# Graph scatter stage: TensorE's bank addresses packed into one word per four pairs, ScalarE's loop over units turned by half a unit

## The reference, cut to what matters

```python
def _spmm(src, dst, w, x, n):
    return jax.ops.segment_sum(w[:, None] * x[src], dst, num_segments=n)
...
msg = h[src] * norm[:, None]
out = jax.ops.segment_sum(msg, dst, num_segments=n_nodes)
```

## Time and profile before

| | us |
|---|---|
| median of 3 runs (2047.58 to 2049.47) | 2048.79 |
| the profiled execution, its own time | 2048.91 |
| the profiled execution, its span | 2047.0 |
| building stage, TensorE's first pair to ScalarE's last instruction | 107.7 to 689.7 |
| TensorE busy over the span | 1791.3 (88%) |
| VectorE busy | 930.7 (45%) |
| ScalarE busy | 605.9 (30%) |

### The profile page before, as it was taken

The page is one execution under the profiler, slowest core; times in us unless marked ns, Lnnn a source line. Parts: engine busy times, 40 slices in busy tenths (PEclk is TensorE's granted clock), DMA queues, the critical chain, the costliest instruction groups (busy, mean ns, idle before and its releaser), DMA issues.

```text
span 2047.0 us, 31184 instructions
## 1 busy us (share of the span) xinstructions
PE 1791.3 (88%) x10360; PEld 1412.7 (69%) x10364; DVE 930.7 (45%) x1708; ACT 605.9 (30%) x1076; POOL 149.8 (7%) x163
## 2 busy tenths in 40 slices
PE   2588988888777799999999999979999999998992
PEld 1288888777676577777777777756667777676871
DVE  5899999788777101111103323332220332235343
ACT  0023567777777410000001111233320000004540
POOL 2000000000000000000000000000000000140354
PEclk8789999899898789999999999989999999999996
DMA  2041133333334854444444343400017434433554
GB/s 86 21 142 80 80 160 160 160 160 160 160 160 195 277 152 137 136 143 144 148 142 128 112 128 114 127 1 0 0 49 247 120 119 125 133 120 117 163 156 138
DMA packets 108624, 260.96 MB, mean 127 GB/s; under 512 B 13005, under 2 KB 65383, under 8 KB 103067
## 3 DMA queue, kind: packets, MB, share of 16 engines
q1 hardware_dynamic: 90874, 240.29, 34.4%
q0 software_dynamic: 5568, 12.82, 2.0%
q10 hardware_dynamic: 12128, 7.16, 1.5%
HBM read 160.44 MB, written 108.04 MB: 131 GB/s over the span
## 4 chain that ended last, share of the span: by engine, by line
issue 53%; PE 29%; ACT 7%; DVE 6%; ACTq 3%; POOL 1%; DMA 1%; DVEq 1%; SPq 0%; POOLq 0%
PE ps L1732 11%; PE ps L1798 5%; PE ps L1733 4%; ACT ps L711 3%; ACT wide L705 3%; PE ps L1993 2%; PE ps L2009 2%; ACTq L696 2%; DVE act_c L1195 1%; PE ps L1704 1%; PE ps L1815 1%; POOL act_c L1016 1%; PE ps L2001 1%; PE ps L1985 1%; DMA act_c<-expert_replies,pair_tab 1%
## 5 line engine op out<-in xcount | busy, mean ns | idle before, releaser
L1732 PE MATMUL ps<-early,act_c 128*128 128x200 bf16 x3600 | 473.0, 261 | 102.9 <-ACT ps L679 57.2
L1798 PE MATMUL ps<-wide 128*128 128x320 f32 (+1 forms) x2000 | 534.8, 428 | 2.9 <-DVE pair_tab L1435 2.9
L1798 PEld LDWEIGHTS ps<-wide 128*128 128x128 f32 x2000 | 379.3, 191 | 145.2 <-DVE pair_tab L1435 3.0
L1732 PEld LDWEIGHTS ps<-early,act_c 128*128 128x128 bf16 x3600 | 343.0, 101 | 135.4 <-issue 127.5
L1733 PE MATMUL ps<-early,act_c 128*128 128x208 bf16 x1200 | 316.6, 264 | 0.0
L1798 PE MATMUL ps<-wide,act_a 128*128 128x320 f32 (+1 forms) x1000 | 268.3, 431 | 8.8 <-ACTq L744 8.8
L1195 DVE TENSOR_TENSOR act_c<-act_c,pair_tab 128x3072 bf16<-128x3072 bf16 x150 | 262.3, 1749 | 0.0
L1798 PEld LDWEIGHTS ps<-wide,act_a 128*128 128x128 f32 x1000 | 192.0, 192 | 82.6 <-issue 11.8
L705 ACT COPY wide<-ps 128x816 f32<-128x816 f32 x200 | 167.1, 836 | 174.5 <-PE ps L1733 135.3
L1299 DVE TENSOR_TENSOR wide<-ps,rows 128x1280 f32<-128x1280 f32 x10 | 14.9, 1492 | 409.1 <-PE ps L1815 409.1
L711 ACT ACTIVATE ps<-ones 128x816 f32<-128x816 f32 x200 | 170.6, 853 | 8.1
(11 more groups left out here) (232 smaller groups left out, 1498.3 us busy)
## 6 DMA issues: line engine op xcount, KB each, us to landing
wide<-weight_matrix SPq DMA_DIRECT2D x90, 800.0 KB, 4.5
weight_matrix<-wide SPq DMA_DIRECT2D x20, 2000.0 KB, 6.2
count_matrix<-wide SPq DMA_DIRECT2D x20, 2000.0 KB, 10.8
wide<-count_matrix SPq DMA_DIRECT2D x45, 800.0 KB, 4.5
expert_replies<-wide SPq DMA_DIRECT2D x63, 128.0 KB, 1.9
wide<-weight_matrix SPq DMA_DIRECT2D x20, 400.0 KB, 3.7
rows<-routed_tokens SPq DMA_DIRECT2D x42, 128.0 KB, 2.3
wide<-count_matrix SPq DMA_DIRECT2D x10, 400.0 KB, 3.9
```

The source lines that it names most:

```text
L1732: nc.tensor.matmul(weights, hot_lane[:, slot, part, two, :, k], hot_key[:, slot, two, 0:WCOLS, k], start=False, stop=True, skip_group_chec ...
L1798: i = nc.tensor.matmul(ps[:, 2 * sub + h, 0:n], features[:, q * QUADS + t, h * P:(h + 1) * P], moving, start=q == 0 and t == 0, stop=q == ...
```

## The change

1. **TensorE's tables.** The 16 offsets and 4 free numbers of a line become 4 words, one for each quad: the free number in bits 0 to 8, and the bank numbers of the four pairs from bit 9 on, three bits each. TensorE's TENSOR_LOAD takes 4 words and not 20. Each pair's bank offset comes from a shift and a mask of its quad's word, and the free number from a mask. VectorE makes the words with four dependent multiply-adds of 300 elements, and no longer shifts the 1200 bank numbers by 9.
2. **ScalarE's loop.** The rows of the end table are moved by five groups. The loop is entered in the middle of a unit: it loads ten ends, takes groups 5 to 9 of a unit, copies the degree row, waits for the next staging buffer and takes groups 0 to 4 of the next unit. The first five groups run ahead of the loop, with a load of five words. The last turn of four units is written out behind the loop. Within it the last four groups are not zeroed again and get no diagonal.
3. **Order of ScalarE's two bodies.** The body for disordered input stands first, the ordered one behind it.

```diff
+BANK_AT = 9
+BANK_BITS = 3
+HALF = UGROUPS // 2
...
-        line_cols = PPAD // LINE * LINE_COLS
-        line_tab = early[0:1, 0:line_cols].bitcast(I32)
+        line_cols = PPAD + PPAD // QUAD
+        bank_tab = early[0:1, 0:PPAD].bitcast(I32)
+        quad_tab = early[0:1, PPAD:line_cols].bitcast(I32)
...
-            with act.If(disordered < 1):
...
             with act.If(disordered > 0):
...
+            with act.If(disordered < 1):
...
+                def take_group(s, u4, k, end, again):
...
+                    act.wait_ge(pair_done, end)
+                    act.copy(stage[half][:, :, k * GCOLS:(k + 1) * GCOLS].rearrange("p r (b j) -> p b r j", b=GROUP),
+                             group_ps.rearrange("p b (r j) -> p b r j", j=WIN)).then_inc(copies_done, 1)
+                    act.wait_ge(copies_done, s * (4 * UGROUPS) + group + 1)
+                    if k == UGROUPS - 1:
+                        act.sem_inc(unit_complete, 1)
+                    if again:
+                        act.activation(group_ps, zero, ACT.Copy, scale=0.0)
+                        act.drain()
+                        self_loops(first_bank, group + SETS, s).then_inc(acc_free, 1)
+
+                def units_of(s, last):
+                    for u4 in range(4):
+                        final = last and u4 == 3
+                        ends = ends_at(s * 4 + u4 + 1, HALF if final else UGROUPS)
+                        for k in range(HALF, UGROUPS):
+                            take_group(s, u4, k, ends[k - HALF], not final or k < UGROUPS - SETS)
+                        degrees_of(u4, u4 % 2, s).then_inc(unit_summed, 1)
+                        if not final:
+                            following = (u4 + 1) % 4
+                            s_of = s + 1 if u4 == 3 else s
+                            stage_free(s_of * 2 + following // 2, following % 2)
+                            for k in range(HALF):
+                                take_group(s_of, following, k, ends[HALF + k], True)
+
+                ends = ends_at(0, HALF)
+                stage_free(0, 0)
+                for k in range(HALF):
+                    take_group(0, 0, k, ends[k], True)
+                with act.Fori(0, SUPERS - 1) as s:
+                    units_of(s, False)
+                units_of(SUPERS - 1, True)
...
-            dve.tensor_single_scalar(bank_tab, bank_tab, 9, op=ALU.logical_shift_left).then_inc(dve_chain, 1)
+            for n in range(QUAD):
+                dve.scalar_tensor_tensor(quad_tab, bank_rows[:, :, n], float(1 << BANK_AT + n * BANK_BITS), quad_tab, ALU.mult, ALU.add).then_inc(dve_chain, 1)
+                dve.wait_ge(dve_chain, count(1))
...
-                        _, (*banks, f0, f1, f2, f3) = nc.values_load_multi_w_load_instructions(
-                            line_tab[:, ds(line * LINE_COLS, LINE_COLS)], engines=(mybir.EngineType.PE,), min_val=0, max_val=(ACCS - 1) * 512,
...
+                        _, quads = nc.values_load_multi_w_load_instructions(
+                            quad_tab[:, ds(line * LINE_QUADS, LINE_QUADS)], engines=(mybir.EngineType.PE,), min_val=1, max_val=(1 << BANK_AT + QUAD * BANK_BITS) - 1,
...
-                        for quad, free in enumerate((f0, f1, f2, f3)):
+                        for quad, word in enumerate(quads):
+                            free = word & (1 << BANK_AT) - 1
...
-                                bank = banks[quad * QUAD + n]
+                                shifted = word >> n * BANK_BITS if n else word
+                                bank = nc.s_assert_within(shifted & (ACCS - 1 << BANK_AT), 0, (ACCS - 1) * 512, skip_runtime_bounds_check_because="three bits from bit BANK_AT on")
```

More of the change, by code:

```diff
@@ L74 @@
 LINE_QUADS = LINE // QUAD
-LINE_COLS = LINE + LINE_QUADS
+BANK_AT = 9
+BANK_BITS = 3
 ENDS = 12
+HALF = UGROUPS // 2
 ACCS = 8
@@ L741, in _, with ends_at @@
                         degrees_of(u4, half, s).then_inc(unit_summed, 1)
+            with act.If(disordered < 1):
+                for b in range(SETS):
+                    act.activation(ps[:, b * GROUP:(b + 1) * GROUP, 0:PCOLS], zero, ACT.Copy, scale=0.0)
+                act.drain()
+                for b in range(SETS):
+                    self_loops(b * GROUP, b, 0).then_inc(acc_free, 1)
+                def ends_at(row, n):
+                    _, ends = nc.values_load_multi_w_load_instructions(
+                        end_tab[:, ds(row * ENDS, n)], engines=(mybir.EngineType.Activation,), min_val=1, max_val=PPAD + SLOTS * BATCH,
+                        skip_runtime_bounds_check_because="the table counts the pairs up to a group's end, and SLOTS * BATCH more")
+                    return ends
+                def take_group(s, u4, k, end, again):
+                    half, group = u4 % 2, u4 * UGROUPS + k
+                    first_bank = group % SETS * GROUP
+                    group_ps = ps[:, first_bank:first_bank + GROUP, 0:PCOLS]
+                    act.wait_ge(pair_done, end)
[6 more added lines that the diff above has]
+                        act.activation(group_ps, zero, ACT.Copy, scale=0.0)
+                        act.drain()
+                        self_loops(first_bank, group + SETS, s).then_inc(acc_free, 1)
[19 more added lines that the diff above has]
+                units_of(SUPERS - 1, True)
@@ L1166, in _ @@
[L1166 to L1170, removed]
+            dve.tensor_scalar_add(quad_tab, quad_tab, 1.0).then_inc(dve_chain, 1)
@@ L1171, in _ @@
+            dve.tensor_scalar_add(end_rows[:, 1:BUNITS, :], starts[:, first_half].rearrange("p (u e) -> p u e", e=UGROUPS), float(SLOTS * BATCH)).then_inc(dve_chain, 1)
+            dve.tensor_scalar_add(end_rows[:, BUNITS, 0:HALF - 1], starts[:, first_half.stop:], float(SLOTS * BATCH)).then_inc(dve_chain, 1)
+            dve.memset(end_rows[:, BUNITS, HALF - 1:HALF], PPAD + SLOTS * BATCH).then_inc(dve_chain, 1)
             dve.tensor_copy(disorder_tab, disorder).then_inc(dve_chain, 1)
-            dve.wait_ge(dve_chain, count(6))
+            dve.wait_ge(dve_chain, count(5))
@@ L1717, in _ @@
                         line = step * (UNROLL * BATCH // LINE) + m
-                        _, (*banks, f0, f1, f2, f3) = nc.values_load_multi_w_load_instructions(
-                            line_tab[:, ds(line * LINE_COLS, LINE_COLS)], engines=(mybir.EngineType.PE,), min_val=0, max_val=(ACCS - 1) * 512,
-                            skip_runtime_bounds_check_because="the table holds (window mod ACCS) * 512, and a group of windows' number plus one")
-                        for quad, free in enumerate((f0, f1, f2, f3)):
+                        _, quads = nc.values_load_multi_w_load_instructions(
+                            quad_tab[:, ds(line * LINE_QUADS, LINE_QUADS)], engines=(mybir.EngineType.PE,), min_val=1, max_val=(1 << BANK_AT + QUAD * BANK_BITS) - 1,
+                            skip_runtime_bounds_check_because="a word holds a group of windows' number plus one and, from bit BANK_AT on, window mod ACCS of four pairs")
+                        for quad, word in enumerate(quads):
+                            free = word & (1 << BANK_AT) - 1
                             batch, half = (m * LINE + quad * QUAD) // BATCH, quad % (BATCH // QUAD)
```

23 lines of the change are left out of this document (13 added, 10 removed).

## The result

| | before | after |
|---|---|---|
| median of four runs, us | 2048.67 | 2089.18 |
| lowest to highest | 2047.58 to 2049.47 | 2088.32 to 2098.33 |
| the profiled execution | 2048.91 | 2098.33 |

A forecast was written before the change was run, and what follows sets the result against it. VectorE was taken to bound units 0 to 8, ScalarE with its slow register load units 9 to 18. 24.0 + 18 + 3.9 - 0.9 + 6.1 - 6.1 = 45.0 us less: 2004 us, own range 1996 to 2012, wider 1996 to 2023.

The forecast's parts named there:

- More address arithmetic: TensorE's sequencer: shift and mask add 0.03 us a pair (bounds nothing to 0.20), hidden below the array's 0.36, costing nothing.
- Rival D: TensorE's sequencer becomes the bound; four separate instructions add 0.20 us a pair, stage 650 us, kernel 2118 us; chance 0.04.
- ScalarE's load at mid-unit: ScalarE's load falls outside a write's slow time, 1.03 us not 3.43; 24.0 us less in units 9 to 18.
- Units 1 to 8: Building stage: waiting above VectorE's 212.6 us mostly goes, 18 us less (bounds 8 and 21).
- Unit 19: Last unit: 2.4 us less for ScalarE's load, 1.1 for its end, 0.4 for TensorE's load; 3.9 us less.
- TensorE's four-word load: TensorE's load takes 0.63 us, 2.1 within a write; its gain lies inside other terms, so nothing is added.
- Rival A: ScalarE's load stays slow at mid-unit, so units 9 to 18 give nothing; 2040 us; chance 0.12.
- The jumps: ScalarE's exchanged bodies: 6.1 us less at the end, 6.1 more at the start; bounds for the sum -4 and +5.
- VectorE's tables: Ahead of the stage: one shift of 1200 goes, four dependent operations on 300 come; +0.9 us (bounds 0.3 and 2).
- Rival B: ScalarE's loop no longer stays in its instruction store, three returns could cost 6.1 us each; 2022 us; chance 0.09.

The follow-up runs named there:

- e6: e2 with one needless mask added to each pair's bank offset on TensorE; 2172.67 us (one run), +90 us to the kernel before on its chip.
- e8: Changed kernel with clamped waits, bank numbers taken out by division and remainder in place of shift and mask; 2046.95 us, ratio 0.9831 to before.
- e2: Kernel before with clamped waits, ScalarE's turned loop and exchanged bodies, TensorE's 20-word tables kept; 2048.69 us, ratio 0.9997 to before.
- e1: Kernel before with only a clamp (larger of value and 1) on loaded values that waits use; 2085.92 us, ratio 1.0189 to before.
- e3: Kernel before, clamped, with only TensorE's packed words by shift and mask, old loop and body order; 2120.15 us, ratio 1.0343 to before.
- e4: e2 with the ordered body first and the disordered one behind it; 2052.98 us, ratio 1.0022 to before.
- e10: e8 with the ordered body first and ScalarE's signal to the engines' meeting given ahead of the jump; 2045.18 us, ratio 0.9820 to before.
- e11: e1 with only the packed words added, taken apart by division and remainder, loop not turned; 2101.27 us, ratio 1.0084 to before.
- e7: e2 with a shift and a mask added for each pair on TensorE; 2265.66 us (one run), +183 us to the kernel before on its chip.

## Why the prediction was wrong

**The step that failed** is "More address arithmetic": "I take 0.03, since one such instruction already holds several operations. It hides below 0.36, and costs nothing." Both halves were wrong. Shift and mask are not taken into the instruction that is there; they cost 0.10 us each, so 0.18 us for the 1.75 of a pair, near the far bound of the step. This alone brings the step to 0.44 us, over the 0.36 it was held against, and decided the result. And the test was made against the wrong figure, as e6 shows, whose step of 0.34 passes it. What the sequencer must stay below is not the array's 0.36 us for a pair but VectorE's 6.5 us for a line, with the load added: 16 steps and a load stand one behind the other. The 16 x 0.1 us of lead between these two figures was what hid the load. The prediction did name this cover ("since it has queued work"), in the step on the load, and did not ask who else would draw on it.

**Rival D** had the mechanism and the formula. For x = 0.20 it gives 8.29 us a line; the trace shows 8.08. Its 2118 us was 29 too much. Its stage of 650 us was 37 too long (730.33 less 116.95 is 613.4): some 16 from the line, and some 16 from the loads within writes, which it priced by 20 words (28 us in all), while the four-word load takes 0.95 us at most. The later start and the longer passes, less the earlier end, made up for 8 of it. It stood at a chance of 0.04, argued down by "the operations of one address sit in one instruction now". The row behind it showed one instruction for the address of that kernel, in which no shift and no mask was asked for.

**ScalarE's load at mid-unit**: right, 0.99 us in place of 3.43. Worth 24 us in units 9 to 18 by the step; with the sequencer out of the way (e8) it is 26.5 together with the packing, 21.1 us a unit where 21.3 was said. But the step gave it to the turn alone, and e2 shows 9.4. That TensorE's long loads come next was missing.

**Units 1 to 8**: 18 us by the step, 13.4 in e8 (233.65 less 220.27), for which VectorE is busy for 212.7; inside the bounds of 8 and 21. **Unit 19**: 3.9 by the step, 3.3 in e8.

**TensorE's four-word load**: 0.63 us estimated, 0.34 measured; in a write 2.1 estimated, 0.95 at most measured. A straight line through 1 and 20 words doesn't hold, since one word takes 0.49 us (the flag, another line of the program) and four take 0.34. **Rival A** is out, and so is the Trainium skill's figure beside it ("Runtime: NRT & Kernel Launch", Instruction fetch mechanics, about 200 ns a register): by it ten words would take 2.0 us and four 0.8, and the rows show 0.99 and 0.34. The page gives its figure for the register loads that the runtime puts around a kernel, and these are loads from SBUF within one.

**The jumps**: +6.1 was 8.35, -6.1 was 6.0; with VectorE's tables (+0.9, right) the start came 9.2 us later. A sum of +2.3, within the bounds of -4 and +5. **Rival B** was not seen in the kernel after, whose turn has 263 instructions, but its mechanism is shown in e1, e3, e4, e10 and e11, at 2.4 to 7.2 us a return.

With its failed step mended, most of the prediction stands: e8, with fused unpacking, is 35.4 us faster than before on its chip. Its passes start 37.3 us earlier by the stage table (+9.0 at the start, +2.9 in unit 0, -13.4, -26.5, -3.3, and -6.0 at the end), where 45.0 was the sum. Taken off 2048.7 that gives 2013 us, just outside the forecast's own range (to 2012) and inside the wider one (to 2023).

## What to carry to other kernels

Before you trade memory traffic for address arithmetic on a sequencer, look at how a register expression is built: multiply, add, divide and remainder went into one instruction here, and shift and mask each became one more, at 0.10 us. Cost a sequencer by the whole round (its steps, its loads, its restarts, in series) against the pace of the engine that it feeds; a gap between its step and the array's is no free room if it already hides a load. And when two slow things lie side by side, test their removal together: in units 9 to 18 the turned loop alone gave about a third of what both gave, and the packing alone less in the one loop where it was tried.

## What the runs showed of the hardware

- An ALU_OP on TensorE's sequencer lasts 32 to 36 ns by the profile and takes 0.10 us of its time (e6, e7). A FUSED_REGOPS with a division and a remainder lasts 135 ns, and the pair's step with it is 0.30 to 0.34 us (e8).
- A register load's price hangs on its words and on the write beside it: 20 words on TensorE 1.36 us, up to 4.7 in a write; 10 words on ScalarE 0.99 and 3.4; 4 words on TensorE 0.34 and up to 0.98 (e3, e11). What the prediction read from the earlier trace rows held in the kernel after too: its 19 long loads start 1.3 to 8.1 us behind a write's issue, the short ones 10.1 us or more, or ahead of all writes.
- A taken jump over about one body on ScalarE shows a gap of 8.2 to 8.9 us at the start (8.86 in e2) and of 2.8 to 7.0 us at the end (2.78 in e4, 5.7 in e10, 6.13 before, 7.0 in e1, e3 and e11). A loop's return is free or costs 2.4 to 7.2 us: free with 256 instructions a turn (before), with 263 (after) and with 299 (e2, e8); 2.4 to 2.6 us with the same 299 at another place (e4); 7 us with 296 (e1, e3, e11). The count of instruction transfers on the page tells which: 22 to 24 without gaps, 38 to 43 with them. The Trainium skill ("Runtime: NRT & Kernel Launch", Instruction fetch mechanics) says that a taken branch whose target isn't among the two pages at hand waits for a fetch; the trace agrees in kind, and that one loop shows both prices at two places fits a limit in pages and not in instructions. No run here moved a loop by single instructions, so where the limit lies is open, and so is why a return costs 2.4 us in one loop and 7 in another, with five transfers a turn in both.
- TensorE's granted clock in units 1 to 18 is 0.93 and 0.91 before, 0.94 and 0.92 in e2, and 1.00 in after and in e8. What raised it was not tested.
